# One pipeline over all head pairs of all batches, with the scores of a pair on two halves of the array

## The chip, the core and the metric

The kernel runs on one core of one Trainium2 chip. A core has five engines that run their own instruction streams and meet at semaphores: TensorE (PE, matrix products into the eight PSUM banks), VectorE (DVE), ScalarE (ACT), GpSimd (POOL) and SyncE (SP, which issues DMAs). The metric is the device time of one execution in microseconds (us); lower is better.

## The reference, cut to what matters

The reference is two transformer layers. What the change touches is the first one's attention on eight batches of 512 rows (16 heads of 64 columns, causal, with a slope per head), and, beside it, the row-wise work that follows it.

```python
x = x + _layernorm(_L0_attn_ref(_layernorm(x), Wq, Wk, Wv, Wo, bo))   # x: 8 x 512 x 256
x = x + _layernorm(_L0_ffn_ref(_layernorm(x), weight, disha))
x = x + _layernorm(_L1_attn_ref(_layernorm(x), ...))
x = x + _layernorm(_L1_ffn_ref(_layernorm(x), ...))                   # 64 experts, 8 per row

def _L0_attn_ref(x, Wq, Wk, Wv, Wo, bo):
    q, k, v = ((x @ W).reshape(b, n, 16, 64) for W in (Wq, Wk, Wv))
    scores = einsum('bihd,bjhd->bhij', q, k) * 64 ** -0.5 + slope * (i - j)
    attn = softmax(where(i >= j, scores, -1e30))
    return einsum('bhij,bjhd->bihd', attn, v).reshape(b, n, 1024) @ Wo + bo
```

## The kernel before, in words

Everything is in fp32. A batch is 512 rows in four tiles of 128. Heads are taken in pairs (hp, 0 to 7), because the 128 columns of one projection block hold two heads.

**Attention of a batch.** `enter` transposes the normalised input (8 transposes of 128x128). PE then projects values (`values`, eight blocks of 128 rows x 512 columns for a batch) and, for each pair, queries and keys (`queries`, `keys`, one block each). A score product needs only 64 rows of the array. Before, `kpad` holds the keys of each head with zeros in the other head's 64 rows, so that one full-height product with both heads' queries gives one head's scores. DVE writes `kpad` with two half-height copies (`k_evac`). Per head there are four products, for the row tiles with 512, 384, 128 and 256 columns that the causal mask leaves; they go to banks 0, 1 and 3.

**From scores to output of a pair.** DVE subtracts the distance, writes `prob` and takes the row maximum (`bias_and_max`, four instructions and `negmax` per head). ACT makes the exponentials (`exps`, four). DVE takes the reciprocal of the sums (`reciprocals`). POOL multiplies (`normalise`, four). PE transposes the ten 128x128 blocks that are left of a head, in three units; ACT copies each unit out (`probs_out`). PE multiplies with the values (`pair_values`: the two heads write to the two halves of the partitions of bank 3, each with 64 columns of weights). ACT copies the result (`o_evac`). After the last pair `leave` multiplies by Wo (32 products for two row tiles, twice).

**Posts.** What follows the attention of batch b (layer norms, feed-forward, second attention, the router of the experts) is cut into 18 points. On PE, points 0, 3, 10 and 15 are eight transposes each, 1, 9 and 11 a product of all rows (`rows_out`), 4 a product of the rows with themselves (gram), 5 to 8 small products on it, 16 the router's logits, 17 the ranks in the middle of `leave`. They are worked off between the head pairs of batch b+1, by `post(p, point)` on PE, ACT and DVE. A norm on DVE is `means` (four statistics, an aggregate, an add), `rsqrt` (ten tiny instructions that depend on each other) and `scale` (four). `x_norm` is the same for the input of the next batch. POOL, after `normalise` of each of the first eight heads, issues four indirect DMAs that send the rows of batch b to their experts (`send_rows`, 32 in all). The DMA queue of SP loads x and stores results of a batch.

**Order.** All orders are written out by hand in the streams. Before, the first batch has no posts. Then a loop runs seven times (`pe.Fori(0, B - 1)`), each time with `enter`, six value blocks, the first scores, and eight pairs: scores of pair hp+1 with the projections of pair hp+2 between the heads, a post, transposes of pair hp, values of pair hp, a post. So the pipeline from scores to values empties at the end of each batch. After the loop the posts of the last batch are mixed with the shared expert, and then the 64 experts run.

## Time and profile before

| | us |
|---|---|
| median of three runs | 2460.95 (2460.45 to 2461.36) |
| the profiled execution | 2460.4 |
| its span, first to last instruction | 2458.7 |
| PE busy | 2292.3 (93%) |
| DVE, ACT, POOL busy | 1173.8 (48%), 813.7 (33%), 836.8 (34%) |
| mean granted TensorE clock | 0.971 |

A row of the profile names the line, the engine, the operation and its tiles. A fp32 product is recorded as two instructions, so a projection block (two products) is `x4` and the scores of a head (four products) are `x8`. In a timeline row the first number is the start, the second how long the merged group took, and the bracket at the end is the idle time of the engine before the group with what ended it.

### The profile page before, as it was taken

The numbers are of one execution on the slowest core, as the hardware profiler recorded it, in microseconds if no ns is written. First come the engines' busy times: TensorE is split into PE (matmuls) and PEld (weight loads), VectorE is DVE, ScalarE is ACT, GpSimd is POOL, SyncE is SP. The second block draws the span as 40 slices with busy tenths as digits, with TensorE's granted clock in tenths as the row PEclk, the third lists the DMA queues.
The fourth block names the chain that finished last, engine by engine and source line by source line (L and its number), as shares of the span: only waits on it lengthen the run. The fifth ranks groups of instructions, "written<-read, shape, count | busy, mean of one in ns | idle before, by whom it ended". The sixth has DMA issues, their size and how long they took to land. (4 is left out here: it accounts for less than half of the span.)

```text
span 2458.7 us, 38420 instructions
## 1 busy us (share of the span) xinstructions
PE 2292.3 (93%) x11988; PEld 1690.5 (69%) x11988; DVE 1173.8 (48%) x4191; ACT 813.7 (33%) x2104; POOL 836.8 (34%) x952
## 2 busy tenths in 40 slices
PE   7988998998998998998999989799999999999997
PEld 3555655665565665665655656589999999999854
DVE  3456675665665765765764644222222222222246
ACT  3635434534534534534534411111111111111110
POOL 3316417417417326336235250512222222222200
PEclk9999999999999999999999999999999999999999
DMA  9200002001000000000000220167777777777522
GB/s 326 62 1 18 1 18 78 7 23 36 9 14 30 9 11 21 17 6 22 17 12 10 81 99 9 37 208 255 236 251 240 254 237 252 240 252 240 155 94 94
DMA packets 99381, 244.75 MB, mean 100 GB/s; under 512 B 20532, under 2 KB 76051, under 8 KB 90976
## 3 DMA queue, kind: packets, MB, share of 16 engines
q1 hardware_dynamic: 73184, 224.34, 25.8%
q0 software_dynamic: 26112, 19.55, 4.8%
q14 instruction: 65, 0.53, 0.1%
q8 instruction: 20, 0.33, 0.1%
HBM read 194.23 MB, written 87.91 MB: 115 GB/s over the span
## 5 line engine op out<-in xcount | busy, mean ns | idle before, releaser
L479 POOL TENSOR_TENSOR prob<-prob,rsum 128x128 f32<-128x128 f32 (+3 forms) x512 | 360.5, 735 | 741.3 <-ACT prob L563 569.1
L1466 PE MATMUL bank<-pT,big_w 128*128 128x160 f32 x3072 | 440.5, 300 | 0.7 <-DVE pT L1051 0.7
L1466 PEld LDWEIGHTS bank<-pT,big_w 128*128 128x128 f32 x3072 | 424.9, 191 | 1.5 <-issue 0.8
L525 POOL DMA_INDIRECT acc<-qT,token_e x128 | 184.4, 1440 | 546.0 <-ACT qT L678 492.1
L773 DVE CUSTOM_DVE_ANT_0 prob<-bank,dist 128x512 f32<-128x512 f32 (+3 forms) x512 | 228.8, 488 | 276.9 <-PE bank L1206 261.2
L484 POOL DMA_INDIRECT disp<-send,slot x288 | 283.5, 985 | 199.0 <-DVE slot L974 114.0
L1206 PE MATMUL bank<-kpad,qT 128*128 128x512 f32 (+3 forms) x1024 | 300.6, 437 | 13.2 <-DVE rawmax L773 13.2
L563 ACT ACTIVATE prob<-prob,negmax 128x512 f32<-128x512 f32 (+3 forms) x512 | 280.4, 550 | 92.0 <-DVE negmax L779 92.0
L1206 PEld LDWEIGHTS bank<-kpad,qT 128*128 128x128 f32 x1024 | 170.1, 190 | 153.3 <-issue 77.7
L1234 PE MATMUL bank<-ident,prob 128*128 128x128 f32 x1280 | 183.7, 293 | 60.3 <-ACT pT L537 36.5
L671 ACT ACTIVATE pT<-bank 128x480 f32<-128x480 f32 x128 | 73.0, 570 | 496.6 <-PE bank L1466 496.6
L1479 PE MATMUL bank<-pT,big_w 128*128 128x160 f32 x1536 | 225.6, 303 | 0.0
L1234 PEld LDWEIGHTS bank<-ident,prob 128*128 128x128 f32 x1280 | 152.6, 149 | 95.4 <-ACT pT L537 46.5
L1479 PEld LDWEIGHTS bank<-pT,big_w 128*128 128x128 f32 x1536 | 210.3, 190 | 2.6
L537 ACT ACTIVATE pT<-bank 128x512 f32<-128x512 f32 (+1 forms) x384 | 174.1, 522 | 61.6 <-PE bank L1234 61.2
L1250 PE MATMUL bank<-pT,v_s 128*64 128x512 f32 (+3 forms) x1024 | 172.5, 484 | 1.0
L1066 DVE TENSOR_TENSOR pT<-pT,bank 128x480 f32<-128x480 f32 x128 | 83.6, 653 | 166.6 <-PE bank L1466 156.4
L1250 PEld LDWEIGHTS bank<-pT,v_s 128*64 128x64 f32 x1024 | 71.0, 150 | 87.5 <-issue 60.1
L1184 PE MATMUL bank<-xT,big_w 128*128 128x512 f32 x256 | 122.9, 603 | 6.9 <-ACT xT L537 6.9
L1073 DVE COPY gram<-bank 128x160 f32<-128x160 f32 x128 | 35.5, 319 | 189.5 <-PE bank L1479 189.5
L1190 PE MATMUL bank<-xT,big_w 128*128 128x512 f32 x256 | 120.3, 592 | 0.0
L1260 PE MATMUL bank<-big_w,oT 128*128 128x256 f32 x512 | 114.1, 381 | 5.9 <-DVE key L961 5.9
(177 smaller groups left out, 2765.1 us busy)
## 6 DMA issues: line engine op xcount, KB each, us to landing
big_w<-ew SPq DMA_DIRECT2D x64, 1536.0 KB, 7.2
big_w<-ew SPq DMA_DIRECT2D x64, 768.0 KB, 5.8
disp<-send SPq DMA_DIRECT2D x1, 10272.0 KB, 35.2
xT<-disp SPq DMA_DIRECT2D x64, 160.5 KB
disp<-send,slot POOLq DMA_INDIRECT x288
xs<-x SPq DMA_DIRECT2D x8, 512.0 KB, 4.4
x<-x SPq DMA_DIRECT2D x8, 512.0 KB, 3.5
x_d<-x SPq DMA_DIRECT2D x8, 512.0 KB, 2.6
```

Source lines behind the costliest of these rows:

```text
L479: i = g.tensor_tensor(pr, pr, rsum[:, n, t:t + 1].to_broadcast([P, COLS[t]]), ALU.mult)
L484: g.indirect_dma_start(out=disp, out_offset=bass.IndirectOffsetOnAxis(ap=slot[:, t, k:k + 1], axis=0), in_=send[:, t, :], in_offset=None, ...
L525: g.indirect_dma_start(out=acc, out_offset=bass.IndirectOffsetOnAxis(ap=idx[:, s:s + 1], axis=0), in_=src, in_offset=None, bounds_check=B ...
L537: return a.activation(dst, src, ACT.Copy)
L563: a.activation(prob[:, n % 4, at_t], prob[:, n % 4, at_t], ACT.Exp, bias=negmax[:, n, t:t + 1], scale=slope(n), accum_out=psumm[:, n, t:t ...
L773: v.tensor_tensor_reduce(out=prob[:, n % 4, P_AT[t]:P_AT[t] + COLS[t]], in0=bank[S_BANKS[u]][:, col:col + COLS[t]], in1=dist[:, N - COLS[t ...
L1184: ins = mm(bank[2][:], wq_s[:, c, hp * P:(hp + 1) * P], xT[:, c], start=(c == 0), stop=(c == C - 1))
L1206: ins = mm(bank[S_BANKS[u]][:, col:col + COLS[t]], qT[:, hp % 2, t * P:(t + 1) * P], kpad[:, hp % 2, s, 0:COLS[t]], start=True, stop=True, ...
L1234: ins = nc.tensor.transpose(bank[T_BANKS[u]][:, col + (t - j) * P:col + (t - j + 1) * P], prob[:, (2 * hp + s) % 4, P_AT[t] + j * P:P_AT[t ...
L1250: ins = mm(bank[3][s * DH:(s + 1) * DH, j * P:N], v_s[:, j, (2 * hp + s) * DH:(2 * hp + s + 1) * DH], pT[:, s, T_AT[j]:T_AT[j] + N - j * P ...
L1466: i = mm(bank[2 * half + 1 - part][:, q * CAP:(q + 1) * CAP], w1[:, c, f * P:(f + 1) * P], xbT[:, c], start=(c == 0), stop=(c == C - 1), s ...
L1479: i = mm(bank[(4, 7)[c]][:, 0:CAP], w2[:, f, c * P:(c + 1) * P], act_e[:, f], start=(f == 0), stop=(f == FC - 1), skip_group_check=True)
```

## The change

1. **Scores.** `kpad` is gone; `kT` holds the keys of both heads, written by one DVE copy. The score product of head s uses rows s*64 to s*64+63 of the array only, and head s writes to bank s. The products of a pair are issued in turn, head 0 and head 1, in three rounds: 512 columns; 384 and 128 columns; 256 columns. A round reuses the bank of the round before, so it waits until DVE has read that (`S_FREED`).
2. **Order on PE.** A step for pair hp is: round 0 of pair hp+1, transposes of head 0 of pair hp, a value block, round 1, transposes of head 1, queries of pair hp+2, round 2, a post (`MID`), values of pair hp, keys of pair hp+2, a value block, a post (`END`). Queries, keys and value blocks share bank 2.
3. **Across batches.** `pair_ahead` goes on into the following batch: steps 6 and 7 hold the queries, keys, four value blocks and first scores of the next batch, step 5 its `enter`. The other four value blocks stand in steps 0 to 3. The loop runs six times and the last iteration is written out.
4. **DVE.** The posts are cut into smaller parts that tables place around the rounds: DVE_PRE before round 0, A after round 0, B after round 1, C after round 2 and before the first reciprocal, D between the two reciprocals, E after the key copy. In a norm behind a product the statistics of the first half start before the second half is there (`bias_and_stats`).
5. **POOL.** The 32 sends stand behind heads 1 to 12 (two or three each) instead of behind heads 0 to 7 (four each).
6. **Points 5 and 6** are one point with two bank pairs.

```diff
-        kpad = sb("kpad", [P, 2, 2, N])
+        kT = sb("kT", [P, 2, N])
+        S_ROUNDS = [[(3, 0)], [(2, 0), (0, 3 * P)], [(1, 0)]]
+        S_FREED = [(-1, 0), (1, 2), (4, 6)]
+        MID = {1: 1, 3: 4, 4: 7, 5: 9, 6: 11, 7: 15}
+        END = {0: 0, 2: 3, 3: 5, 4: 8, 5: 10, 7: 16}
+        DVE_C = {0: (0.4,), 1: (1,), 2: (3, 3.5), 5: (9,), 6: (11,)}
+        DVE_D = {0: (0.6,), 1: (1.5,), 4: (7,), 5: (9.5,), 6: (11.5,)}
...
+        def pair_ahead(i, hp, d, following):
+            if hp + d < HP:
+                return i, hp + d
+            return (following, hp + d - HP) if following else None
...
-            SENDERS = H // 2
+            FIRST_SENDER, SENDERS = 1, 12
...
+            def score_round(i, hp, r):
+                if r == 0:
+                    pe.wait_ge(k_ready, at(i, HP, hp + 1))
+                for t, col in S_ROUNDS[r]:
+                    for s in range(2):
+                        freed = hp * S_OPS + S_FREED[r][s]
+                        if (t, col) == S_ROUNDS[r][0] and past(i, H * T, freed):
+                            pe.wait_ge(biased, at(i, H * T, freed))
+                        rows = slice(s * DH, (s + 1) * DH)
+                        ins = mm(bank[S_BANKS[s]][:, col:col + COLS[t]], qT[rows, hp % 2, t * P:(t + 1) * P],
+                                 kT[rows, hp % 2, 0:COLS[t]], start=True, stop=True, skip_group_check=True)
...
+            def step(i, hp, p, following):
+
+                one, two = pair_ahead(i, hp, 1, following), pair_ahead(i, hp, 2, following)
+                if one:
+                    score_round(*one, 0)
+                if p and hp == 4:
+                    pe.wait_ge(t1_ready, at(p, 3 * KS, 3 * KS))
+                if hp == 6 and following:
+                    pe.wait_ge(xT_ready, at(following, C, C))
+                head_transposes(i, hp, 0)
+                if hp < T:
+                    if hp == 0:
+                        pe.wait_ge(v_ready, at(i, 2 * T, HALF))
+                    pe.wait_ge(k_ready, at(i, HP, hp + 2))
+                    values(i, HALF + hp)
+                elif hp >= 6 and following:
+                    if hp == 6:
+                        pe.wait_ge(k_ready, at(i, HP, HP))
+                    else:
+                        pe.wait_ge(v_ready, at(following, 2 * T, 2))
+                    values(following, 2 * (hp - 6))
+                if one:
+                    score_round(*one, 1)
+                head_transposes(i, hp, 1)
+                if two:
+                    if hp < T:
+                        pe.wait_ge(v_ready, at(i, 2 * T, HALF + hp + 1))
+                    elif hp < 6:
+                        pe.wait_ge(k_ready, at(i, HP, hp + 2))
+                    else:
+                        pe.wait_ge(v_ready, at(following, 2 * T, 2 * (hp - 6) + 1))
+                    queries(*two)
+                if one:
+                    score_round(*one, 2)
+                if p and hp in MID:
+                    post(p, MID[hp])
+                pair_values(i, hp)
+                if two:
+                    keys(*two)
+                if hp >= 6 and following:
+                    pe.wait_ge(k_ready, at(two[0], HP, two[1] + 1))
+                    values(following, 2 * (hp - 6) + 1)
+                if hp == 5 and following:
+                    enter(following)
+                if p and hp in END:
+                    post(p, END[hp])
...
+            with pe.Fori(0, B - 2) as b:
+                iteration((b, 1), (b, 0), (b, 2))
+            iteration((None, B - 1), (None, B - 2), None)
```

PE in the first batch, one pair, before (`kpad,qT` are scores, `xT,big_w` with L1184 queries and with L1190 keys, `ident,prob` transposes, `pT,v_s` values):

```order
L1206 MATMUL bank<-kpad,qT 128x512
L1206 MATMUL bank<-kpad,qT 128x384
L1206 MATMUL bank<-kpad,qT 128x128
L1206 MATMUL bank<-kpad,qT 128x256
L1184 MATMUL bank<-xT,big_w 128x512 x2
L1206 MATMUL bank<-kpad,qT 128x512
L1206 MATMUL bank<-kpad,qT 128x384
L1206 MATMUL bank<-kpad,qT 128x128
L1206 MATMUL bank<-kpad,qT 128x256
L1190 MATMUL bank<-xT,big_w 128x512 x2
L1234 MATMUL bank<-ident,prob 128x128 x20
L1250 MATMUL bank<-pT,v_s 64x512 x2
```

The same place now (L1242 is a value block, L1248 queries, L1255 keys):

```order
L1269 MATMUL bank<-kT,qT 128x512 x2
L1285 MATMUL bank<-ident,prob 128x128 x10
L1242 MATMUL bank<-big_w,xT 128x512 x2
L1269 MATMUL bank<-kT,qT 128x384 x2
L1269 MATMUL bank<-kT,qT 128x128 x2
L1285 MATMUL bank<-ident,prob 128x128 x10
L1248 MATMUL bank<-xT,big_w 128x512 x2
L1269 MATMUL bank<-kT,qT 128x256 x2
L1297 MATMUL bank<-pT,v_s 64x512 x2
```

The scores of a pair were one block per head; they now come in three rounds, and between them stand the transposes of the pair before and one projection block each.

DVE in the last batch, step 1, where the norm behind the first feed-forward product stands. Before, it lay whole between the two reciprocals of a pair (the nine other instructions of `rsqrt` are left out here and below):

```order
L783 RECIPROCAL rsum<-psumm 128x4
L708 BN_STATS stats<-bank 128x6 x4
L712 BN_AGGR mv<-stats 128x2 x4
L714 TENSOR_SCALAR vare<-mv 128x4
L719 TENSOR_SCALAR rstd<-vare 128x4
...
L812 TENSOR_SCALAR y<-bank,mv,rstd 128x256 x4
L783 RECIPROCAL rsum<-psumm 128x4
```

Now:

```order
L823 TENSOR_SCALAR negmax<-rawmax 128x4
L751 BN_STATS stats<-bank 128x6 x4
L755 BN_AGGR mv<-stats 128x2 x4
L757 TENSOR_SCALAR vare<-mv 128x4
L827 RECIPROCAL rsum<-psumm 128x4
L762 TENSOR_SCALAR rstd<-vare 128x4
...
L872 TENSOR_SCALAR y<-bank,mv,rstd 128x256 x4
L827 RECIPROCAL rsum<-psumm 128x4
```

The statistics moved ahead of the first reciprocal of the pair (`rsum`), for which POOL waits; the ten instructions of `rsqrt` and the scaling stayed between the two.

## Rows read from the trace of the kernel before

**Rows 1.** The page, busy time, share of the span and instructions of each engine
```profile
PE 2292.3 (93%) x11988; PEld 1690.5 (69%) x11988; DVE 1173.8 (48%) x4191; ACT 813.7 (33%) x2104; POOL 836.8 (34%) x952
```

**Rows 2.** Windows between the ends of `leave`: length, busy of each engine, clock, DMA
```profile
163.80:342.05 178.25, 163.48 (x764) 105.37 (x762) 114.56 (x417) 81.05 (x223) 76.89 (x96) 0.97 0.04 13
521.17:700.77 179.60, 165.65 (x763) 106.89 (x762) 114.19 (x417) 81.18 (x223) 76.72 (x96) 0.95 0.06 20
1239.74:1418.72 178.98, 165.16 (x764) 106.83 (x763) 109.41 (x394) 82.47 (x224) 78.56 (x98) 0.96 0.10 36
```

**Rows 3.** Timeline of PE: five value blocks; one pair with its projections; a post
```profile
528.20 8.75 PE L1170 MATMUL bank<-big_w,xT 128*128 128x512 f32 x20
...
610.98 2.32 PE L1206 MATMUL bank<-kpad,qT 128*128 128x512 f32 x8
613.14 1.88 PE L1184 MATMUL bank<-xT,big_w 128*128 128x512 f32 x4
...
617.01 1.88 PE L1190 MATMUL bank<-xT,big_w 128*128 128x512 f32 x4
...
620.51 2.65 PE L1234 MATMUL bank<-ident,prob 128*128 128x128 f32 x20
623.15 2.37 PE L1250 MATMUL bank<-pT,v_s 128*64 128x512 f32 x16
625.45 0.71 PE L1323 MATMUL bank<-sbd,a_qT 128*128 128x128 f32 x4
```

**Rows 4.** Timeline of PE: posts (gram, rows out) and half of `leave`
```profile
589.43 3.75 PE L1294 MATMUL bank<-xn 128*128 128x258 f32 x16
...
634.65 3.62 PE L1260 MATMUL bank<-mix,xTp 128*128 128x256 f32 x16
...
685.38 7.13 PE L1260 MATMUL bank<-big_w,oT 128*128 128x256 f32 x32
```

**Rows 5.** Timeline of PE: waits, and what followed each
```profile
579.79 2.40 PE L1234 MATMUL bank<-ident,prob 128*128 128x128 f32 x10 [0.78 <-ACT pT L537]
...
671.48 2.40 PE L1234 MATMUL bank<-ident,prob 128*128 128x128 f32 x10 [3.55 <-ACT pT L537]
```

**Rows 6.** Windows of 5 us: length, busy of each engine, granted clock
```profile
580.00:585.00 5.00, 3.15 (x15) 2.75 (x15) 3.57 (x12) 1.95 (x5) 4.23 (x5) 0.50 0.14 48
...
670.00:675.00 5.00, 3.52 (x14) 2.53 (x16) 4.61 (x16) 3.64 (x11) 4.68 (x8) 0.53 0.26 105
```

**Rows 7.** Timeline of DVE: a norm, one beside POOL, and a pair's maximum and reciprocal
```profile
529.01 1.41 DVE L708 BATCH_NORM_STATS2 stats<-x 128x6 f32<-128x256 f32 x4
...
531.18 0.17 DVE L719 TENSOR_SCALAR rstd<-vare 128x4 uint32<-128x4 uint32 x1
...
533.16 1.38 DVE L812 TENSOR_SCALAR xn<-x,mv,rstd 128x256 f32<-128x256 f32 x4
...
578.39 0.14 DVE L719 TENSOR_SCALAR rstd<-vare 128x4 uint32<-128x4 uint32 x1
...
582.60 1.38 DVE L812 TENSOR_SCALAR xn<-x,mv,rstd 128x256 f32<-128x256 f32 x4
...
618.09 0.17 DVE L779 TENSOR_SCALAR negmax<-rawmax 128x4 f32<-128x4 f32 x1
...
620.37 0.18 DVE L783 RECIPROCAL rsum<-psumm 128x4 f32<-128x4 f32 x1
```

**Rows 8.** Timeline of ACT: first and last exponential of one head
```profile
618.29 0.72 ACT L563 ACTIVATE prob<-prob,negmax 128x512 f32<-128x512 f32 x1 [0.37 <-DVE negmax L779]
...
620.00 0.49 ACT L563 ACTIVATE prob<-prob,negmax 128x256 f32<-128x256 f32 x1
```

**Rows 9.** Timeline of POOL: `normalise` of three heads, four sends behind the first two
```profile
578.56 2.74 POOL L479 TENSOR_TENSOR prob<-prob,rsum 128x128 f32<-128x128 f32 x4 [0.92 <-DVE rsum L783]
...
602.67 2.75 POOL L479 TENSOR_TENSOR prob<-prob,rsum 128x128 f32<-128x128 f32 x4 [8.48 <-ACT prob L563]
610.42 2.74 POOL L479 TENSOR_TENSOR prob<-prob,rsum 128x128 f32<-128x128 f32 x4
```

More of the change, by code:

```diff
@@ L48, in at, with past @@
     return k * per + n if reg is None else reg * per + (k * per + n)
+def past(i, per, n):
+    reg, k = i
+    return reg is not None or k * per + n > 0
 def index(i):
@@ L783, in reciprocals, with step, posts @@
                 v.reciprocal(rsum[:, n, :], psumm[:, n, :]).then_inc(rsum_ready, 1)
-            def heads(i, hp, p=None):
-                bias_and_max(i, 2 * hp)
-                if p is not None:
-                    post(p, 2 * hp - 1.5)
-                bias_and_max(i, 2 * hp + 1)
-                if hp + 1 < HP:
-                    k_evac(i, hp + 1)
-                reciprocals(i, 2 * hp)
+            def step(i, hp, p, following):
+                one, two = pair_ahead(i, hp, 1, following), pair_ahead(i, hp, 2, following)
+                def posts(table):
+                    if p:
+                        for part in table.get(hp, ()):
+                            post(p, part)
+                posts(DVE_PRE)
+                if one:
+                    bias_and_max(*one, 0)
+                posts(DVE_A)
+                if one:
+                    bias_and_max(*one, 1)
+                posts(DVE_B)
+                if one:
+                    bias_and_max(*one, 2)
+                posts(DVE_C)
+                if one:
+                    reciprocals(one[0], 2 * one[1])
+                posts(DVE_D)
+                if one:
+                    reciprocals(one[0], 2 * one[1] + 1)
+                if two:
+                    k_evac(*two)
+                posts(DVE_E)
+                if hp == X_NORM_AT and following:
+                    x_norm(following)
             count = [0]
@@ L852, in post @@
                     in_order()
-                    norm(xn_t, lambda t: x1[:, t, :], normed)
+                elif point == 0.4:
+                    means(did, in_order, lambda t: x1[:, t, :], stats_p, mv_p, vare_p)
+                elif point == 0.6:
+                    rsqrt(did, in_order, vare_p, rstd_p, newton_p)
+                    scale(xn_t, lambda t: x1[:, t, :], normed)
                 elif point == 1:
                     dve.wait_ge(rows_psum, at(p, ROWS, 2))
-                    norm(y_t, rows)
+                    means(did, in_order, rows, stats_p, mv_p, vare_p)
+                elif point == 1.5:
+                    rsqrt(did, in_order, vare_p, rstd_p, newton_p)
+                    scale(y_t, rows)
                 elif point == 2:
@@ L900, in post @@
                         dve.wait_ge(rows_psum, at(p, ROWS, 3 + j))
-                        add_bias(j, bqs_b)
-                    in_order()
-                    norm(xn_t, y_t, normed)
+                        bias_and_stats(j, bqs_b)
+                    aggregate()
+                elif point == 9.5:
+                    rsqrt(did, in_order, vare_p, rstd_p, newton_p)
+                    scale(xn_t, y_t, normed)
                 elif point == 11:
@@ L908, in post @@
                         dve.wait_ge(rows_psum, at(p, ROWS, 5 + j))
-                        add_bias(j, l1bo_b)
-                    in_order()
-                    norm(y_t, y_t)
+                        bias_and_stats(j, l1bo_b)
+                    aggregate()
+                elif point == 11.5:
+                    rsqrt(did, in_order, vare_p, rstd_p, newton_p)
+                    scale(y_t, y_t)
                 elif point == 13:
```

394 lines of the change are left out of this document (192 added, 202 removed).

## The prediction

> **What bounds the kernel now.** I read the page first, for the shares: PE is busy 93% of the span, no other engine half of it [rows 1]. Then the windows, to see which part of the span the change reaches. The first batch ends at 163.8 us, seven loop iterations follow up to 1418.7 (1254.9 in all, 179.3 each), and the shared expert and the experts, which the change leaves alone but for the order of a few posts, take the rest [rows 2]. In an iteration PE is busy 165.7 of 179.6 us and DVE 114. So about 14 us are waits, and part of the busy time is slow: after a wait of 3.55 us ten transposes took 2.40 us [rows 5] where they take 1.3 [rows 3], and PE's granted clock was 0.50 to 0.53 there [rows 6], its lower level of 1.2 GHz.
>
> Then the timeline of PE, for the price of each block. By the starts of neighbours: a projection block 1.72 (8.75 us for five, and 613.14 to 614.86 as the head's scores behind end at 617.01, 2.15 later) [rows 3]. Scores of a head take 2.15, twenty transposes 2.64 (1.3 a head), values of a pair 2.30, `rows_out` 3.45, gram 3.58, half of `leave` 7.0 (the 0.17 by which a group outlasts the start of the next is its tail) [rows 3, 4].
>
> **What two halves of the array are worth.** The scores of a head stream 1280 columns in 2.15 us, and there are 128 such blocks in the kernel. The values of a pair are two heads of 1280 columns each, on two column halves, and take 2.30, not 4.3 [rows 3]. So halves of columns run side by side, at 0.15 for going in and out. The trace has no pair on two row halves. Bounds: 2.15 for a pair if they overlap fully, 4.3 if they don't at all. I take the values' row, which is nearest, with its 0.15 paid in each of the three rounds: 1.0, 1.0 and 0.6, 2.6 for a pair against 4.3. That removes 1.7 x 8 = 13.6 us of PE work per batch.
>
> The Trainium skill (TensorEngine Tiling (Array Packing), Key Properties) says that a change of tiling mode drains TensorE, which speaks against three rounds: six changes a pair more than before. By the row above that is the 0.15 a round which the sum already holds; by the rule alone, which gives no figure, it could be more.
>
> **The new pipeline, step by step.** PE's own work in a loop iteration would be some 147 us (165.7 busy, less 13.6, less about 5 by which the low clock stretched blocks [rows 2, 5]). What has to be checked is the chain that runs once per step: round 2 of a pair, then DVE, ACT, DVE, POOL, then this pair's transposes in the next step, and behind them round 2 of the pair after it. Its links: from the end of a score block (617.01) to the end of `negmax` 1.25 [rows 3, 7], of which 1.0 is left where only 256 columns are open; exponentials of a head 2.2, 618.29 to 620.49 [rows 8]; reciprocal to POOL 0.3 [rows 7, 9]; so POOL starts 3.5 after round 2. POOL takes 2.75 for a head, and with four sends behind it the next head starts 7.75 after it (602.67 to 610.42) [rows 9], 1.2 to 1.3 a send: 6.45 with three, 5.2 with two, 2.9 with none. Then PE: transposes 1.3, queries 1.7, round 2 0.6, and waits for semaphores 0.15.
>
> That gives the least length of a step. With three sends: 3.5 + 6.45 + 2.75 + 0.15 + 3.6 = 16.5. With two: 15.2. With none, over head 0's transposes: 3.5 + 2.9 + 0.15, then 1.3, value block 1.7, round 1 1.0 and 3.6 again, 14.1; without a value block 12.4. PE's work in a step is 11 to 21 by its posts, on average (147 - 15 of `leave`) / 8 = 16.5. So the sends and the chain are longer than PE's work in the short steps, and posts on DVE lie inside the chain. DVE prices: means 2.2 (529.01 to 531.18), rsqrt 2.0 (to 533.16), scale 1.35; beside POOL's `normalise` an rsqrt took 4.2 (578.39 to 582.60), and POOL had started at 578.56 [rows 7, 9]. In the new order the rsqrt of part D starts together with POOL, which the same reciprocal releases, so I charge 4.0 for it there. From the end of round 2 to the next one:
>
> - Step 0: means, reciprocal, rsqrt at 4.0 and scale lie behind the two maxima, so the transposes of `END` start 10.5 late; PE waits 6.5 us. With 0.9, 1.0, 1.3, 1.7, 1.0, 1.3, 1.7, 0.6 behind it: 20.0.
> - Step 1: the first reciprocal waits for `rows_out` 3.45 and means; the second comes after rsqrt and a scale from PSUM (5.9): 18.5.
> - Step 2: rsqrt and scale ahead of the reciprocals, 1.6 longer than the exponentials cover: 18.0.
> - Step 3: PE's own work, gram 3.6, values, keys, 5.2 for point 5: 20.4.
> - Step 4: `x_norm` (5.5, and 1.8 more beside POOL) lies ahead of round 0's maxima, and round 1 needs those banks: 20.2.
> - Step 5: as step 0, behind `rows_out`: 20.7. Step 6: the same, and 3.4 of point 13 ahead of the maxima: 20.9.
> - Ahead of the first round 2: 8.6. Behind the last: 24.4, of which `leave` 14.0.
>
> Sum 171.7, against 179.3. The work removed is 13.6, but 7.6 comes back; the rest goes into waits for DVE and POOL, about 29 where 14 were.
>
> **First batch and last.** Eight blocks ahead of the first scores as before, so scores at 32.7. The rounds there wait for DVE each (4.9), the chain adds 12.8 to the first round 2 of step 0 (50.4), then 3 x 14.1, 12.8, 18.3 with `x_norm`, 2 x 14.1, 5.7 of rest and 2.9 + 13.8 up to the end of `leave`: 174.4 against 163.8. That holds 14.7 of the next batch's projections. The last iteration has none of those, no `x_norm` and no projections in steps 6 and 7: 14.2 less than the others, 157.5.
>
> **Sum.** 174.4 + 6 x 171.7 + 157.5 = 1362.1, against 1418.7: 56.6 less. The last batch's first norm starts on half of its rows, one add and two statistics earlier, 1.4. Together 58 less than the profiled execution's 2460.4, which lies 0.5 under the median: 2402. The single copy of the keys (one of 0.7 instead of two) and the memset of `kpad` stand beside PE's work and count nothing. Nor does the second copy of the loop's body in code: loading it stands beside 170 us of work; if it did not, one wait of some us. SP's queue gets the same DMAs, its early loads wait for keys and transposes that now come sooner, and `sent` on POOL moves from head 8 to head 13, long ahead of the norm that needs it in step 7. The low clock I charge at nothing beyond what iterations have now: each of the two waits of today costs 1.1 to 1.6 in the blocks behind it, and in the new order such blocks partly stand ahead of a wait anyway. If it is charged on five waits of 2.5 us and more, 1.6 x 5 = 8 per iteration.
>
> **Rivals.**
>
> 1. *The chain hides better than I walked it* (PE-bound). The DVE parts beside POOL lose nothing (4 x 1.9 an iteration), and half of the other waits close as the steps shift against each other. For it: today's iteration has only 14 us of waits with similar posts. Against it: step 0 alone is 17 us of DVE work in a row. An iteration of 158: 7 x 13.7 = 96 less, 2306.
> 2. *The clock takes the gain.* Every step has a wait, several of 3 us or more, and after such waits the row shows the lower level [rows 5, 6]. At 8 us per iteration, 7 x 8 = 56: 2458, no change or slightly faster. The Trainium skill (TensorE: Matmul & The Clock Gate, Why this matters for your kernels) has the rule that idle gaps between bursts of matmuls bring the half rate back; by that rule, the trace agrees, this rival is likelier the more of my waits are real.
> 3. *Row halves don't overlap* (slower). Place: the three rounds. Each pair then costs 4.45 to 4.75 and not 2.6, on PE between links of the chain, so nearly all of it shows: 1.9 x 64 = 120, 2522. It decides from 0.9 us per pair on, where the 58 are used up. This is also the case in which the change doesn't do what it says. For it: each round's second head waits for a bank of its own, and a round is short. Against it: the values' row.
>
> **Chances.** Forecast 0.60, rival 1 0.17, rival 2 0.13, rival 3 0.10. A difference of under 0.2% (5 us) can't be told from none. Rival 2 splits into 0.05 faster, 0.05 same and 0.03 slower. So faster 0.60 + 0.17 + 0.05 = 0.82, same 0.05, slower 0.10 + 0.03 = 0.13. Range: down into rival 1 and up to rival 2, 2310 to 2462. The forecast's own is 2365 to 2440.
>
> **What would show it.** Step by step, in the profile after: the scores' rows of a pair in round 0 take 1.0 (right) or 1.8 us (rival 3). An iteration, from `leave` to `leave`, is near 172 us; at 158 rival 1 holds, near 179 rival 2, with PE's clock under 0.93. DVE's rsqrt of step 0 takes 4 us beside POOL, and PE waits about 6 us for `xn` ahead of the `END` transposes of step 0. PE waits for POOL (`prob`) at the transposes of head 1 in steps 0 to 5. The first batch ends later than now, near 174. I would be wrong if the waits stood elsewhere, or if the time after the loop moved by more than some us.

## The result: 2557.4 us, 3.9% slower

The changed kernel took 2557.43 us (2554.71 to 2560.52), the kernel before, timed with it, 2461.15 us: a ratio of 1.039, 95% interval 1.0372 to 1.0408. The forecast was 2402 and the range ended at 2462: wrong in sign.

### The profile after

The page of the changed kernel (span 2558.8 us), its line of busy times, to set beside [rows 1]:

```profile
PE 2259.5 (88%) x11988; PEld 1612.4 (63%) x11988; DVE 1135.9 (44%) x4127; ACT 812.7 (32%) x2104; POOL 840.3 (33%) x951
```

PE's busy time fell by 32.8 us, the span rose by 100.1, so PE is idle for 133 us more.

Windows of the changed kernel from one end of `leave` to the next, an iteration of the loop and the last batch's, to set beside [rows 2]:

```profile
580.45:771.34 190.89, 159.23 (x764) 95.26 (x763) 109.80 (x409) 80.85 (x223) 77.63 (x96) 0.94 0.05 19
...
1344.71:1516.08 171.37, 142.29 (x708) 89.81 (x708) 97.53 (x364) 73.28 (x200) 71.36 (x88) 0.91 0.10 37
```

An iteration takes 191 us where 171.7 were forecast and 179.3 were needed before. Six of them are 118 us of the error of 155. The first batch ends at 196.3 (174.4 forecast), the last takes 171.4 (157.5), and what lies behind it 1042.7 (before 1040.0).

What PE waited for, whole program, in the changed kernel (us in total, times, longest):

```profile
PE bank L1367 <- DVE xn L872: 77.6, 22, 6.7
PE bank L1269 <- DVE kT L804: 46.8, 20, 5.0
PE bank L1242 <- DVE kT L804: 42.1, 14, 4.5
PE bank L1269 <- DVE rawmax L816: 38.8, 9, 5.6
PE bank L1285 <- POOL prob L511: 30.3, 17, 5.0
```

and in the kernel before:

```profile
PE bank L1234 <- ACT pT L537: 36.5, 21, 3.6
PE bank L1273 <- DVE xn L812: 30.1, 15, 6.8
PE bank L1234 <- DVE kpad L762: 22.3, 13, 2.6
PE bank L1206 <- DVE rawmax L773: 13.2, 13, 1.8
```

The five kinds make 235.6 us, the four of before 102.1: the difference, 133.5, accounts for the idle time above. The largest that the forecast did not have is the wait for `kT`, the key copy: 88.9 us, ahead of round 0 (L1269) and of the value blocks of steps 6 and 7 (L1242).

One such place, steps 0 and 1 of a loop iteration. The timeline of PE in the changed kernel (start, length, what it is; in brackets the idle time ahead and who ended it):

```profile
599.82 1.97 PE L1367 MATMUL bank<-ident,xn 128*128 128x128 f32 x8 [6.37 <-DVE xn L872]
601.72 2.08 PE L1269 MATMUL bank<-kT,qT 64*128 64x512 f32 x4
...
611.40 3.72 PE L1354 MATMUL bank<-weff,xTp 128*128 128x256 f32 x16
...
617.36 1.98 PE L1255 MATMUL bank<-xT,big_w 128*128 128x512 f32 x4
624.34 2.18 PE L1269 MATMUL bank<-kT,qT 64*128 64x512 f32 x4 [4.99 <-DVE kT L804]
```

and of DVE in the same stretch:

```profile
617.44 0.18 DVE L827 RECIPROCAL rsum<-psumm 128x4 f32<-128x4 f32 x1
...
617.70 0.41 DVE L765 TENSOR_TENSOR newton<-rstd 128x4 f32<-128x4 f32 x1
618.15 0.54 DVE L767 SCALAR_TENSOR_TENSOR newton<-newton,vare 128x4 f32<-128x4 f32 x1
618.72 0.75 DVE L770 SCALAR_TENSOR_TENSOR rstd<-newton,rstd 128x4 f32<-128x4 f32 x1
619.50 0.96 DVE L765 TENSOR_TENSOR newton<-rstd 128x4 f32<-128x4 f32 x1
...
621.49 1.90 DVE L872 TENSOR_SCALAR y<-bank,mv,rstd 128x256 f32<-128x256 f32 x4
623.42 0.18 DVE L827 RECIPROCAL rsum<-psumm 128x4 f32<-128x4 f32 x1
623.51 0.69 DVE L804 COPY kT<-bank 128x512 f32<-128x512 f32 x1
```

The key projection is done at 619.3. Its copy is the last of DVE's row of work in the step, behind an inverse root, a scaling and the second reciprocal, and starts at 623.5; round 0 follows it. The first batch has no such parts and shows the same gate at its least:

```profile
88.14 0.18 DVE L827 RECIPROCAL rsum<-psumm 128x4 f32<-128x4 f32 x1 [1.73 <-ACT prob L591]
90.31 0.18 DVE L827 RECIPROCAL rsum<-psumm 128x4 f32<-128x4 f32 x1 [2.00 <-ACT prob L591]
90.41 0.66 DVE L804 COPY kT<-bank 128x512 f32<-128x512 f32 x1
```

DVE sits waiting for ACT's exponentials (2.00 us) with the key copy queued behind that wait. PE pays for it twice here: it waits 1.94 us, and blocks behind the wait run at the lower clock (ten transposes 2.39, where they take 1.31 otherwise; granted clock 0.66 from 91 to 96 us):

```profile
91.12 1.37 PE L1269 MATMUL bank<-kT,qT 64*128 64x512 f32 x4 [1.94 <-DVE kT L804]
92.42 2.39 PE L1285 MATMUL bank<-ident,prob 128*128 128x128 f32 x10
...
97.83 1.31 PE L1285 MATMUL bank<-ident,prob 128*128 128x128 f32 x10
```

The second payment isn't certain. The first batch has seven waits of 1.94 to 1.95 us for this copy, and behind two of them, at 76.21 and 177.49 us, the clock stayed at 1.00.

The mean granted clock was 0.949 in the changed kernel and 0.971 before. The trace has only two levels of it, 1.0 and 0.5; a mean m of them puts a share 2(1 - m) of the span at the lower one, so 261 us against 143.

### The profile page after: what moved, and what is told of

Its sections match the earlier page's. It is cut to its first block and busy times, and to the rows that moved or that the text cites. A ratio compares the mean times of both kernels' runs of the same rounds, so it can differ in the third digit from the quotient of the medians.

```text
span 2558.8 us, 38192 instructions
## 1 busy us (share of the span) xinstructions
PE 2259.5 (88%) x11988; PEld 1612.4 (63%) x11988; DVE 1135.9 (44%) x4127; ACT 812.7 (32%) x2104; POOL 840.3 (33%) x951
## 3 DMA queue, kind: packets, MB, share of 16 engines
q1 hardware_dynamic: 73184, 224.34, 24.8%
## 5 line engine op out<-in xcount | busy, mean ns | idle before, releaser
L516 POOL DMA_INDIRECT disp<-send,slot x288 | 289.2, 1004 | 274.1 <-DVE slot L1067 194.2
L1269 PE MATMUL bank<-kT,qT 64*128 64x512 f32 (+3 forms) x1024 | 231.1, 535 | 85.6 <-DVE kT L804 46.8
L1269 PEld LDWEIGHTS bank<-kT,qT 64*128 64x128 f32 x1024 | 99.5, 206 | 226.5 <-issue 134.9
L1285 PEld LDWEIGHTS bank<-ident,prob 128*128 128x128 f32 x1280 | 158.7, 156 | 110.4 <-issue 84.3
L1285 PE MATMUL bank<-ident,prob 128*128 128x128 f32 x1280 | 191.3, 303 | 33.0 <-POOL prob L511 30.3
L1242 PE MATMUL bank<-big_w,xT 128*128 128x512 f32 x256 | 132.0, 641 | 42.1 <-DVE kT L804 42.1
L1297 PE MATMUL bank<-pT,v_s 128*64 128x512 f32 (+3 forms) x1024 | 153.5, 442 | 0.0
L1248 PE MATMUL bank<-xT,big_w 128*128 128x512 f32 x256 | 128.6, 627 | 1.7 <-ACT xT L571 1.7
L1255 PE MATMUL bank<-xT,big_w 128*128 128x512 f32 x256 | 126.7, 618 | 0.0
```

The source lines that it names most:

```text
L516: g.indirect_dma_start(out=disp, out_offset=bass.IndirectOffsetOnAxis(ap=slot[:, t, k:k + 1], axis=0), in_=send[:, t, :], in_offset=None, ...
L1269: ins = mm(bank[S_BANKS[s]][:, col:col + COLS[t]], qT[rows, hp % 2, t * P:(t + 1) * P], kT[rows, hp % 2, 0:COLS[t]], start=True, stop=True ...
L1285: ins = nc.tensor.transpose(bank[T_BANKS[u]][:, col + (t - j) * P:col + (t - j + 1) * P], prob[:, (2 * hp + s) % 4, P_AT[t] + j * P:P_AT[t ...
L1297: ins = mm(bank[O_BANK][s * DH:(s + 1) * DH, j * P:N], v_s[:, j, (2 * hp + s) * DH:(2 * hp + s + 1) * DH], pT[:, s, T_AT[j]:T_AT[j] + N - ...
```

## The experiments

The theories. K: the key copy's place on DVE holds round 0, and so each step. D: the later layers' pieces, ahead of whose transposes PE waits for `xn`, and the input normalisation ahead of round 0's maxima hold the iteration. C: the lower clock behind the waits costs by itself. P: the path exponentials, reciprocals, POOL, transposes is as long as the step, whatever else is moved. Ratios are to the kernel before in the same job; "iteration" is from one end of `leave` to the next in the loop.

**1. The key copy between the two reciprocals.**

```diff
+                if two:
+                    k_evac(*two)
                 posts(DVE_D)
                 if one:
                     reciprocals(one[0], 2 * one[1] + 1)
-                if two:
-                    k_evac(*two)
```

> The changed kernel, with DVE's copy of the keys moved from behind the second reciprocal to between the two, ahead of the D parts. Theory K (round 0 waits for the key copy, which stands behind the second head's exponentials and the D parts): the waits of 4.99 and 4.45 us ahead of round 0 of step 2 and of the value block of step 7 go, and a plain step goes from 14.9 to about 14.1, where POOL's first head takes over; 6 to 9 us less per loop iteration, 5 less in the first batch, 45 to 65 in all, so 2495 to 2512. Theory C (the low clock after waits is what costs): the waits are only moved, under 15 us in all.

Measured 2549.75, 1.0361 (1.0344 to 1.0378). The waits for `kT` fell from 88.9 to 20.9 us, and the first batch ended 12.3 us earlier (183.9), a plain step in 13.99. But an iteration stayed at 191.2: PE waited for `xn` 88.8 (77.6), for `prob` 43.5 (30.3). Of the 45 to 65 us expected, 8 came. K holds in the first batch and not by itself in the loop, where other gates were right behind it.

**2. Products that nobody reads ahead of step 0's transposes.**

```diff
+                if p and hp == 0:
+                    for _ in range(FILL):      # FILL = 7
+                        mm(bank[PA][:], ident[:], dist[:], start=True, stop=True, ..)
```

> The changed kernel, with seven products of 512 columns into a bank that nobody reads, issued on PE in step 0 ahead of the END transposes, where PE waits 6.4 us for the norm. They take about 6 us, so the wait is filled and the clock is not lost. Theory C: the eight transposes behind it take 0.9 and not 1.9 us and round 0 takes 1.06 and not 2.0, about 2 us less per iteration, 14 in all, 2543. If the low clock there is hidden behind a later wait (for the key copy or POOL), no change within 5 us. Theory K alone says no change.

Measured 2575.85, 1.0463: 18 us slower than the change, where 14 faster or no change was expected. Step 0 itself was 1.6 us shorter, but iterations were up to 5 us longer (192.8 to 196.0), at a mean clock of 0.946 (0.949). The trace shows where: the lower clock had gone from step 0 and turned up elsewhere, above all in step 7. There PE waits 1.91 us for the key copy in both kernels. In the changed kernel the clock stays at 1.00 behind it, in this one the same blocks run slower, and the stretch behind the last round 2 takes 29.6 us where it took 26.3. First the changed kernel, then this one:

```profile
752.30 1.98 PE L1242 MATMUL bank<-big_w,xT 128*128 128x512 f32 x4 [1.91 <-DVE kT L804]
754.12 1.90 PE L1436 MATMUL bank<-wg_s,hT 128*128 128x64 f32 x16
755.85 7.13 PE L1354 MATMUL bank<-big_w,oT 128*128 128x256 f32 x32
```

```profile
755.15 2.75 PE L1243 MATMUL bank<-big_w,xT 128*128 128x512 f32 x4 [1.91 <-DVE kT L805]
757.70 3.51 PE L1440 MATMUL bank<-wg_s,hT 128*128 128x64 f32 x16
761.00 8.15 PE L1358 MATMUL bank<-big_w,oT 128*128 128x256 f32 x32
```

So one filled wait can cost more than it gives; no run here shows what decides whether a wait of 1.9 us lowers the clock.

**3. The scores over all 128 rows, order unchanged** (each product then sums both heads, so the values are not the reference's; it is run for its time).

```diff
-  ins = mm(bank[..], qT[rows, hp % 2, ..], kT[rows, hp % 2, 0:COLS[t]], ..)
+  ins = mm(bank[..], qT[:, hp % 2, ..], kT[:, hp % 2, 0:COLS[t]], ..)
```

> The changed kernel, with the score products over all 128 rows of the array (the two heads' scores come out summed, so the values are others; the shapes, the order and all copies are the same). It undoes the two halves alone. If halves overlap as the rows say (1.06, 1.07, 0.63 us a round) and the rounds lie on the chain: 1.55 us more for each of the 64 pairs, 100 us more, 2657. If the rounds' time is hidden by the waits for DVE and POOL, under 30 us more.

Measured 2584.04, 1.0497: 26.6 us more, where PE's rounds have some 100 us more to do (4.3 against 2.76 a pair). The rest came back in two ways. PE's busy time rose by 49.8 only, as its other blocks took 48 less: the clock was 0.961 (0.949), so some 60 us less of the span lay at the lower level, and blocks beside a round are shorter when all products use 128 rows (experiment 11). And PE's idle time fell by 26. So about half of what the halves save had gone into slower neighbours and a quarter into waits.

**4. Both heads' transposes behind the three rounds**, the pT copies on ACT likewise, and the key projection ahead of the pair's values.

> The changed kernel, with another order in the step: the three rounds with the projection blocks between them first, then both heads' transposes, keys, post, values; ACT's copies in the same order. The chain from round 2 over DVE, ACT and POOL to the next step's transposes then has the whole tail of the step and the next three rounds to pass, about 12.6 us where it needs 6.5 to 9.3, so a plain step should be PE's own 12.3 to 13 us and not 14.9 to 16.5. Theory K': the place of the rounds around the transposes is what made the chain a step long; an iteration comes to 165 to 172 us (step 0 still waits for its norm), the first batch to about 175, in all 2410 to 2440. Theory D (DVE's posts in the step are the bound): an iteration stays at 182 or more, 2500.

Measured 2634.29, 1.0699, where 2410 to 2440 or 2500 was expected, and a plain step took 16.9. ACT's exponentials now stood behind six copies, and with them the reciprocals, the first of which waits 4.13 us here (1.73 in the changed kernel), and the key copy:

```profile
82.79 2.77 ACT L571 ACTIVATE pT<-bank 128x512 f32<-128x512 f32 x6 [0.53 <-PE bank L1285]
85.43 0.73 ACT L591 ACTIVATE prob<-prob,negmax 128x512 f32<-128x512 f32 x1
```

```profile
87.74 0.18 DVE L827 RECIPROCAL rsum<-psumm 128x4 f32<-128x4 f32 x1 [4.13 <-ACT prob L591]
```

My reorder lengthened the chain it was meant to relieve. It says nothing for or against P.

**5 to 7. Theory D.** The four pieces at the ends of steps 0, 2, 4 and 5 (transposes, mixing product) moved on PE and ACT into the next step, ahead of round 1 (behind the value block where there is one), with the key copy of experiment 1; then the input normalisation cut in three; then the sends as in the kernel before.

```diff
-        END = {0: 0, 2: 3, 3: 5, 4: 8, 5: 10, 7: 16}
+        EARLY_POST = {1: 0, 3: 3, 5: 8, 6: 10}
+        END = {3: 5, 7: 16}
...
                     values(following, 2 * (hp - 6))
+                if p and hp in EARLY_POST:
+                    post(p, EARLY_POST[hp])
```

> The key copy between the two reciprocals (as in the first experiment) and, beside it, four pieces of the batch before's later layers moved on PE and ACT from the end of a step to the middle of the next one, behind its value block: the transposes of the FFN's, layer 1's and layer 1's output input, and the mixing product. Theory D (the normalisations on DVE are not ready when the end of the step asks for them, and everything queued on PE behind those transposes waits too): the waits for xn, 88.8 us with the key copy alone, fall under 20 us, an iteration goes from 191 to 179-182 us, time 2465-2490. Theory P (the path of exponentials, reciprocals, POOL and transposes of the next pair is as long as the step, whatever stands at its end): the waits turn up again for prob and kT, iteration 188 us or more, time 2530 or more.

> As the kernel with the posts later, and the normalisation of the next batch's input, one piece of some 5.5 us behind step 4's reciprocals, cut in three: its statistics behind round 0's D minus in step 4, its inverse root behind round 1's, its scaling alone where the whole stood. Theory D: the waits for rawmax, 42.2 us with the key copy alone, fall under 15 us (first batch too), time 25 to 35 us below the kernel with the posts later. Theory P: less than 10 us below it.

> As the kernel with the split input normalisation, and the sends of a batch's rows again four behind each of the first eight heads instead of two or three behind twelve. If the sends between the heads set when the transposes can start, the waits for prob change by 10 us or more either way and the time with them; if POOL has room, the time stays within 8 us of that kernel.

Measured 2465.94 (1.0011), 2445.55 (0.9936) and 2459.99 (0.9993). The waits for `xn` fell to 7.6 us, an iteration to 180.9 and, with the cut, 177.5. With the key copy moved, D holds for both its parts, and P falls (it had an iteration at 188 or more). The cut was worth 20 us, a little under the 25 to 35 expected: the waits for `rawmax` fell from 62.6 to 45.1 only. The sends four behind eight heads cost 14 us (the waits for `prob` rose from 43.1 to 57.7); in this order, then, their spreading is a gain.

**8. The pieces later, the key copy left where the change put it.**

> The changed kernel with nothing but the four later-layer pieces moved to the middle of the next step; the key copy stays behind both reciprocals and both D parts. With the key copy moved as well the time was 2466, with the key copy moved alone 2550, with neither 2557. If the waits for the normalisations are the larger loss and the two add up, 2557 - (2550 - 2466) = 2473; if the key copy behind the D parts then holds the path in the steps that have D parts (theory K: about 46.8 us of waits stand there), 2490 to 2520.

Measured 1.0449 (1.0432 to 1.0467), an iteration 194.6: worse than the change itself, where 2473 to 2520 us was expected. PE and DVE of that kernel in step 0:

```profile
605.69 2.18 PE L1272 MATMUL bank<-kT,qT 64*128 64x512 f32 x4 [7.38 <-DVE kT L807]
```

```profile
603.39 1.51 DVE L875 TENSOR_SCALAR xn<-x,mv,rstd 128x256 f32<-128x256 f32 x4
604.83 0.16 DVE L830 RECIPROCAL rsum<-psumm 128x4 f32<-128x4 f32 x1
604.91 0.65 DVE L807 COPY kT<-bank 128x512 f32<-128x512 f32 x1
```

The same DVE work that had held the transposes by 6.4 us now holds round 0 by 7.4. Up to the end of the last `leave`, which leaves out what differs between chips (see below), the changed kernel takes 1516 us. The key copy moved alone gives 8 less, the pieces moved alone 19 more, both together 92 less. Two gates stood behind one queue of DVE work, and each hid the other.

(Experiments 8 to 11 shared a chip on which the kernel before took 2503 us; experiment 15 met another such chip, 2507 us. In the traces taken there the part behind the last `leave` took 1078 us, elsewhere 1039 to 1043. Ratios and iterations are compared.)

**9 to 11. Another order inside the step; two DVE pieces off the path; the halves undone there.** On PE: round 0, value block, first transposes, round 1, query projection, second transposes, round 2, key projection, values; on DVE, against experiment 6:

```diff
+                if two:
+                    k_evac(*two)
                 if one:
                     reciprocals(one[0], 2 * one[1])
-                if two:
-                    k_evac(*two)
                 posts(DVE_D)
```

> The kernel with the split input normalisation (2445.6), with another order inside a step: on PE round 0, the value block, the first head's transposes, round 1, the query projection, the second head's transposes, round 2, the key projection, the pair's values; the key copy on DVE ahead of the first reciprocal. The waits for kT, 39.5 + 11.0 us there, should go, and the transposes stand up to 1.8 us later than the exponentials need. Theory D: 40 to 60 us faster, 2385 to 2405. Rival (the path round 2, exponentials, POOL, second transposes, round 2 is as long as the step): the waits for prob, 43.1 us, grow by as much, within 12 us of 2446.

> As the keys-first kernel, with two pieces on DVE taken from ahead of a round 0: the scaling of the next batch's input behind round 0 of step 5, the statistics of point 13 behind round 0 of step 7 (its inverse root and scaling behind round 1). The waits for rawmax, 45.1 us with the split input normalisation, should fall under 25 us: 10 to 20 us below the keys-first kernel; if they only move to prob, within 5 us of it.

> As the keys-first-spread kernel, with the score products over all 128 rows of the array (heads mixed, so what comes out is not the reference's): in the changed kernel that cost 27 us only. The three rounds' matmuls last 4.3 us instead of 2.76 a pair, 98 us for 64 pairs. If the path is PE's own work now, 70 to 100 us slower than the keys-first-spread kernel; if the waits still hide the halves, under 40 us.

Measured 0.9622, 0.957 (0.9554 to 0.9586) and 0.9641; iterations of 166.7, 165.9 and 167.2 us. The order gave more than the 40 to 60 us expected: up to the end of the last `leave` 72 us less than experiment 6. The waits for `kT` fell from 50.5 to 22.5 us and those for `prob` from 43.1 to 25.3, so the rival, P once more, fell too. What of it is PE's order, what ACT's copies, which follow it, and what the place of the key copy, was not taken apart. In the second kernel, PE behind round 2 of a step, and DVE beside it:

```profile
564.84 1.88 PE L1269 MATMUL bank<-xT,big_w 128*128 128x512 f32 x4
566.65 2.37 PE L1311 MATMUL bank<-pT,v_s 128*64 128x512 f32 x16
...
574.33 1.13 PE L1283 MATMUL bank<-kT,qT 64*128 64x512 f32 x4
```

```profile
566.75 0.69 DVE L813 COPY kT<-bank 128x512 f32<-128x512 f32 x1 [3.90 <-PE bank L1269]
```

Here the copy waits for PE and not PE for the copy; it lies beside the pair's values. Waits for `kT` of up to 1.8 us are left in 14 steps.

Undoing the halves there cost 16.4 us, far under the 70 to 100 expected. PE's busy time rose by 49.8 (2206.5 to 2256.3), and not 100. By the starts of neighbours, up to the last `leave`, the rounds took 89 us more and all other blocks 37 less. One reason is the blocks beside a round on halves: a projection block behind one takes 1.82 against 1.71 from start to start, ten transposes ahead of one 1.19 against 1.09; the first fence is of the kernel with halves, the second of the one without:

```profile
608.17 1.98 PE L1256 MATMUL bank<-big_w,xT 128*128 128x512 f32 x4
609.99 1.26 PE L1299 MATMUL bank<-ident,prob 128*128 128x128 f32 x10
```

```profile
618.07 1.88 PE L1256 MATMUL bank<-big_w,xT 128*128 128x512 f32 x4
619.78 1.25 PE L1299 MATMUL bank<-ident,prob 128*128 128x128 f32 x10
```

The other is the lower clock, which covers 28 us less without them (0.981 against 0.975), up to 14 us of work. How the 37 divide between the two was not measured. Against the 49.8, PE's idle time fell by 34.4 (the waits for `kT`, `rawmax` and `prob` took 68.9 us with halves, 41.4 without).

**12. The keys-first order alone on the changed kernel**, pieces and input normalisation left as the change has them.

> The changed kernel with only the keys-first order inside a step (round 0, value block, first transposes, round 1, query projection, second transposes, round 2, key projection, the pair's values; the key copy ahead of the first reciprocal); the later layers' pieces stay at the ends of the steps and the input normalisation stays whole. With both moved as well the order gave 166.8 us an iteration. If the order inside a step was the whole loss, about 170 us an iteration, 0.97 of before. If the pieces at the ends hold an iteration by themselves (their waits for xn, 77.6 to 88.8 us, and for rawmax, 38.8 to 42.2, come on top), 183 to 187 us an iteration, 1.01 to 1.03 of before. If nothing changes without the pieces moved, as with the key copy alone, 190 us and 1.036.

Measured 2516.64, 1.0227 (1.021 to 1.0244), an iteration 187.6, about as the second case said (183 to 187): the waits for `xn` were 88.7 us and for `rawmax` 74.4.

**13. Four waits of an iteration filled with products nobody reads** (steps 0, 1, 6 and 7).

```diff
+        FILL = {0: (PA, 7), 1: (4, 5), 6: (4, 5), 7: (4, 2)}
...
                 if two:
                     keys(*two)
+                if p and hp in FILL and (hp < 6 or following):
+                    for _ in range(FILL[hp][1]):
+                        mm(bank[FILL[hp][0]][:], ident[:], dist[:], start=True, stop=True, ..)
```

> The changed kernel with products that nobody reads put on PE where it waits longest in a loop iteration: 7 of 512 columns behind the key projection of step 0 (into bank 6), 5 behind that of step 1, 5 of step 6 and 2 of step 7 (into bank 4). They fill the waits of 6.4, 5.0, 4.5 and 1.9 us and nothing else. Theory C (the lower clock behind those waits costs by itself): the stretches at 1.2 GHz fall from 264 us to 150-180 and the time by 30 to 60 us, 0.015 to 0.025 off the ratio of 1.039. Theory W (the waits are the cost, the low clock runs in time that the next wait swallows): within 10 us of the changed kernel.

Measured 2529.67, 1.0282 (1.0265 to 1.0299): 28 us less than the changed kernel, though PE was busy 74 us longer (2333.6). PE of that kernel at the wait of 4.99 us shown above:

```profile
608.76 4.46 PE L1345 MATMUL bank<-dist,ident 128*128 128x512 f32 x10
613.92 1.23 PE L1270 MATMUL bank<-kT,qT 64*128 64x512 f32 x4 [0.71 <-DVE kT L805]
615.08 1.31 PE L1286 MATMUL bank<-ident,prob 128*128 128x128 f32 x10
```

The gate is the same, the copy; the work behind it runs at 2.4 GHz (round 0 1.23 and not 2.18). The mean clock was 0.967, so 167 us at the lower level instead of 261. C holds: the lower clock costs by itself, 28 us for 94 us of it, just under the 30 to 60 expected. Not every filled wait paid where it stood: steps 0, 1 and 6 became some 1.6 us shorter or more, step 2, which was not touched, 1.7 longer.

**14 to 17. Two more waits taken off the best kernel** (key copy of steps 0 and 2 ahead of part C, the router's transposes later), then both on one chip.

> As the keys-first-spread kernel (0.957 of before), with the key copy of steps 0 and 2 ahead of the normalisation parts that stand behind round 2 (14 waits of up to 1.8 us for kT there) and the transposes of the router's input behind the pair's values instead of ahead of the key projection in step 7 (waits for send, 16.4 us in all). If the rest of the waits adds to the path: 10 to 20 us faster, 0.949 to 0.953. If the first of two waits only hands its time to the next: within 5 us, 0.955 to 0.959.

> The keys-first-spread kernel once more, on a chip where the kernel before takes its usual time (it took 2503 where this kernel was timed first, all of it behind the batches: the span after the last batch was 1078 us there and 1042 elsewhere). If its iterations of 165.9 us are its own, about 2358 us and 0.958 of before, 30 us faster than the kernel with the two further waits taken (2388.6); if they owe something to that chip's clock (0.99 there in the loop, 0.96 with the two further waits taken), 170 us an iteration, within 8 us of 2388.6.

> The keys-first-spread kernel beside the one with two further waits taken, on one chip. If the order makes the difference of the iterations (165.9 against 170.7 us, seen on two chips), this one is 25 to 35 us faster than the other; if the chip made it, they are within 10 us of one another.

> The kernel with the two further waits taken, on the same chip as the keys-first-spread kernel. If taking the waits for kT and send only hands their time to the waits for prob and to a lower clock, it is 25 to 35 us slower than that kernel; if the chip made the difference, within 10 us of it.

Measured 0.9708 (0.949 to 0.953 was expected of a gain, 0.955 to 0.959 of none), 0.9576, and on one chip 2361.89 (0.958, 0.9556 to 0.9603) and 2389.64 (0.9703, 0.9686 to 0.9719). The order makes the difference, not the chip: the kernel with the two waits taken is 28 us slower. In it the waits for `kT` are gone, but those for `prob` stand at 50.8 us where they were 24.0, and 16.4 us for `send` have become 15.0 for `hT`. The lower clock covers some 15 us more (0.972 against 0.975 in the profiled executions; the others of the faster kernel had up to 0.985). Why is open.

The best version of this study is the keys-first-spread kernel: 2361.9 us, 4.2% faster than before and, across chips, 7.6% faster than the change.

## Why the prediction was wrong

Its steps in the profile after, from the end of one round 2 to the next, in the iteration from 580.45:

| stretch | forecast | measured | what was missed |
|---|---|---|---|
| ahead of the first | 8.6 | 8.7 | |
| step 0 | 20.0 | 22.2 | lower clock behind the wait for `xn` |
| step 1 | 18.5 | 23.3 | key copy, 4.99, and the clock behind it |
| step 2 | 18.0 | 18.2 | |
| step 3 | 20.4 | 20.5 | |
| step 4 | 20.2 | 24.3 | lower clock behind 5.6 us for `rawmax` |
| step 5 | 20.7 | 22.7 | lower clock, wait 2.6 |
| step 6 | 20.9 | 24.6 | key copy, 4.45, and the clock |
| behind the last | 24.4 | 26.3 | key copy, 1.9 |

**The step that failed** is "the single copy of the keys ... stand[s] beside PE's work and count[s] nothing". It is on the path. I had followed the chain from round 2 to POOL and the transposes and left out its other branch: both reciprocals, key copy, round 0. In the kernel before, the copy stood ahead of the reciprocals; the change put it last on DVE, and the key projection last on PE. I took a copy of 0.7 us for its own length and not for the queue that it stands in. It made a plain step of the first batch 14.8 to 16.6 us instead of 14.1; with the copy moved (experiment 1) it was 13.99. In the iteration above its three waits are 11.3 of the 19 us missed. But it isn't the whole of the miss in the loop: with it moved the iteration stayed 191.2, and steps 0, 5 and 6 took 23.2, 24.8 and 25.4 where the forecast has 20.0, 20.7 and 20.9. So the steps that hold long pieces of the later layers were priced too low as well, by 3 to 5 us each, waits and lower clock together. Undone together, copy and pieces are worth 92 us (experiments 1, 5, 8).

**The second** is "the low clock I charge at nothing". My own rival 2 had it at 8 us an iteration. In the iteration above the granted clock stood at the lower level for 23.9 us, up to 12 us of work; not all of it shows in the time, as the next wait can swallow it. Experiment 13 gives 3.6 (191.4 to 187.8) for four of the waits; in step 4, which it did not fill, three blocks behind the wait took 2.68, 2.40 and 2.64 where they take 1.14, 1.31 and 1.88, 3.4 us longer in all:

```profile
689.73 2.68 PE L1269 MATMUL bank<-kT,qT 64*128 64x384 f32 x8 [5.62 <-DVE rawmax L816]
692.34 2.40 PE L1285 MATMUL bank<-ident,prob 128*128 128x128 f32 x10
694.53 2.64 PE L1248 MATMUL bank<-xT,big_w 128*128 128x512 f32 x4
```

The rows to price it from stood there before [rows 5, 6].

**What was right.** Row halves overlap: the rounds took 1.06, 1.07 and 0.63 by the starts of neighbours, against 1.0, 1.0 and 0.6, so rival 3 fell. Not in the sum was what the switches cost the neighbours. In a step of the first batch a projection block ahead of a round took 1.81 and ten transposes behind one 1.15, where the kernel of experiment 3 has 1.72 and 1.09 in the same places; from round 0 to the end of round 2 the halves saved 1.45 us (8.68 for 10.13), not the 1.7 of the forecast. The Trainium skill (TensorEngine Tiling (Array Packing), Key Properties) says that a change of mode drains TensorE. The rows fit that, with 0.06 to 0.11 us on either side of a round. The wait for `xn` in step 0 was 6.4 (6.5 forecast), the inverse root beside POOL about 4, steps 2 and 3 within 0.2. POOL's `prob`, for which I expected waits in steps 0 to 5, cost 30 us in the whole program. And one sum of the forecast doesn't hold: it speaks of about 29 us of waits in an iteration, while 171.7 less its own 147 is 25; measured were 31.7.

**The first batch** (196.3 for 174.4) missed the same gate: 12.3 by experiment 1. Of the rest, cutting `x_norm`, which stands ahead of round 0's maxima, gave 3.9 (experiments 5 and 6, 182.4 to 178.5), and the orders of experiments 9 and 10 brought it to 172.1 and 167.1.

**Where the gain went.** The scores by line, before and after (instructions, busy us and mean ns, idle time ahead):

```profile
L1206 PE MATMUL bank<-kpad,qT 128*128 128x512 f32 (+3 forms) x1024 | 300.6, 437 | 13.2 <-DVE rawmax L773 13.2
```

```profile
L1269 PE MATMUL bank<-kT,qT 64*128 64x512 f32 (+3 forms) x1024 | 231.1, 535 | 85.6 <-DVE kT L804 46.8 <-DVE rawmax L816 38.8
```

The halves took 69.5 us off; longer blocks beside them and the lower clock gave 37 back on PE's other work; idle time added 133. The forecast iteration, 171.7, was within reach of the same pipeline: 165.9 with the changes of order of experiments 5, 6, 9 and 10.

## What to carry to other kernels

Before an order is called good, walk every branch that leaves an in-order engine and ask what stands ahead of it in that queue: a copy of 0.7 us behind a reciprocal that waits for exponentials is a gate. Take late gates away in pairs; one alone may show nothing or the wrong sign, since the next one stands in the same queue. And charge each new wait of TensorE for the slower blocks behind it, from the rows that already show them, as a cost that may or may not come: the same wait of 1.91 us cost nothing in one kernel and some 3 us in another.

## What the runs showed of the hardware

- Two row halves of the array run fp32 products side by side, at some loss: four products of 512 columns took 1.06 us, where 128 rows took 1.72, half of which is 0.86. The three rounds of a pair took 2.76 for 4.32. Blocks on either side of a round were 0.06 to 0.11 us longer.
- Waits of 1.9 us were in some places followed by the lower clock (ten transposes 2.39 and not 1.31) and in others not (five of seven in the first batch; in step 7 not in the changed kernel, but in that of experiment 2). Products that nobody reads made a program 28 us faster in four waits an iteration, and 18 us slower in one.
- DVE's instructions with two inputs, of four columns each, took 0.41, 0.54, 0.75 and 0.96 us beside POOL's four of 128, 256, 384 and 512 columns (0.39, 0.61, 0.82 and 1.03 us), and 0.16 when POOL was done: each seems to wait for one whole instruction of POOL. The Trainium skill (SBUF — State Buffer, SBUF: two separate sides) states that the port pair which DVE and GpSimd share is held for a whole instruction; the rows agree.
- Two of the chips ran the part behind the batches 36 us longer (1078 for 1042) and the loop as fast (165.9 us an iteration on both, 166.9 on the chip of experiment 16). In the kernel of experiment 10, 28.8 us of it are four waits of PE ahead of the shared expert's products (L1518); their cause is open.
